# Eleven more matmuls on a zero tile around TensorE's branch, in the opening of an attention and feed-forward kernel

## The reference

```python
q, k, v = x @ Wq.T, x @ Wk.T, x @ Wv.T * sigmoid(x @ Wg.T)   # 16 query heads, 4 key heads, 8 wide
q, k = rotary(rms_norm(q)) * q_gain, rotary(rms_norm(k))
# each head is split in halves; two causal softmax attentions a1, a2
y = concat([a1 - lam * a2, a1 + lam * a2])
x = layernorm(x + y @ Wo.T)
gf = global_net(mean of x over the tokens)                    # small MLP
for _ in range(3):
    tf = coupling_net(x_ffn)                                  # four dense layers
    x_ffn = x_ffn + coupling(gf, tf) * twist(x_ffn)
out = layernorm(x + x_ffn)
```

## Time and profile before

| what | value |
|---|---|
| runs | 264.01, 264.76 and 271.02 us |
| median | 264.76 us |
| profiled execution, its own time | 266.62 us |
| its span, first to last instruction | 264.8 us |
| TensorE busy, share of the span | 234.5 us, 89% |
| VectorE | 206.1 us, 78% |
| ScalarE | 218.8 us, 83% |
| GpSimd | 95.9 us, 36% |
| mean granted clock of TensorE | 0.962 of 2.4 GHz |

### The profile page before, as it was taken

How to read it: one execution, slowest core, us unless ns; L and a number is a source line. 1 busy time by engine, 2 the same in 40 slices (tenths; PEclk the granted TensorE clock), 3 DMA queues, 4 the chain that set the end, 5 groups by cost and what they waited for, 6 DMA issues and landing times.

```text
span 264.8 us, 10915 instructions
## 1 busy us (share of the span) xinstructions
PE 234.5 (89%) x4240; PEld 127.9 (48%) x4240; DVE 206.1 (78%) x747; ACT 218.8 (83%) x316; POOL 95.9 (36%) x225
## 2 busy tenths in 40 slices
PE   8459799997799999999999999899998899998980
PEld 3143456654465564565665554544643222223980
DVE  1789667997878899899899989943442967999992
ACT  3367699997968999999999999999766697777785
POOL 7730323444534354444453553522203000000573
PEclk9957799999979999999999999999999999999997
DMA  4304252461717535346264353381201345651045
GB/s 120 85 1 77 46 121 62 88 133 32 159 42 102 112 85 120 82 96 128 70 119 101 82 114 73 67 156 16 60 12 43 80 102 136 160 122 37 24 138 159
DMA packets 58223, 23.60 MB, mean 89 GB/s; under 512 B 42929, under 2 KB 56145, under 8 KB 58193
## 3 DMA queue, kind: packets, MB, share of 16 engines
q1 hardware_dynamic: 57904, 23.16, 40.9%
q10 hardware_dynamic: 288, 0.02, 0.1%
HBM read 4.96 MB, written 2.10 MB: 27 GB/s over the span
## 4 chain that ended last, share of the span: by engine, by line
PE 31%; DVE 25%; issue 15%; DMA 11%; POOL 10%; ACT 4%; SPq 1%; POOLq 1%; DVEq 1%; ACTq 0%
DMA qk<-parts 9%; PE S L767 7%; DVE roped L1206 3%; PE S L777 2%; PE O L648 2%; DVE rest L1234 2%; PE S L808 2%; POOL root_sq L1603 2%; PE O L635 2%; DVE X L1326 2%; DVE stats L1331 2%; ACT h L1037 2%; DVE parts L1232 2%; POOL root_sq L1595 2%; DVE parts L1236 2%
## 5 line engine op out<-in xcount | busy, mean ns | idle before, releaser
L948 ACT ACTIVATE probs_past<-S 128x1024 f32<-128x1024 f32 x64 | 64.0, 1037 | 3.9 <-PE S L506 3.8
L948 ACT ACTIVATE probs_late<-S 128x1024 f32<-128x1024 f32 x64 | 62.3, 1028 | 4.0 <-PE S L537 3.2
L635 PE MATMUL O<-probs_past,values 128*32 128x512 f32 x256 | 35.0, 618 | 1.2 <-issue 0.6
L648 PE MATMUL O<-probs_late,mixed 128*32 128x128 f32 x512 | 27.4, 286 | 0.0
L648 PE MATMUL O<-probs_late,values 128*32 128x128 f32 x512 | 27.1, 282 | 0.0
L1466 DVE SCALAR_TENSOR_TENSOR cY<-coup,ratio,Y 128x256 f32<-128x256 f32 x48 | 21.1, 481 | 6.3 <-ACT coup L1046 3.8
L767 PE MATMUL S<-X,cn_w 128*128 128x512 f32 x48 | 25.0, 627 | 0.0
L1595 POOL TENSOR_TENSOR root_sq<-estimate 128x40 f32<-128x40 f32 x16 | 6.8, 424 | 40.8 <-DVE estimate L1194 36.7
L516 PEld LDWEIGHTS S<-qk 32*128 32x128 bf16 x512 | 7.6, 92 | 27.9 <-issue 27.9
L1206 DVE TENSOR_TENSOR roped<-rotated,rstd 128x128 f32<-128x128 f32 (+1 forms) x64 | 15.6, 299 | 6.8 <-POOL rstd L1605 6.8
L506 PE MATMUL S<-qk 32*128 32x512 bf16 x128 | 13.7, 412 | 7.9 <-DMA qk<-parts 7.2
(11 more groups left out here) (190 smaller groups left out, 585.3 us busy)
## 6 DMA issues: line engine op xcount, KB each, us to landing
Y<-X SPq DMA_DIRECT2D x48, 128.0 KB, 2.3
xT_in<-in_xT SPq DMA_DIRECT2D x16, 128.0 KB, 2.7
x_res<-in_x SPq DMA_DIRECT2D x16, 128.0 KB, 2.4
out<-result SPq DMA_DIRECT2D x16, 128.0 KB, 1.9
qk<-parts SPq DMA_TRANSPOSE x15, 4.9
future_in<-in_future SPq DMA_DIRECT2D x1, 176.0 KB, 2.8
w_o<-in_w_o SPq DMA_DIRECT2D x2, 64.0 KB, 2.4
cn_w<-in_cn_w SPq DMA_DIRECT2D x2, 64.0 KB, 2.1
```

The lines of the kernel that those rows point to most:

```text
L635: mm = pe.matmul(O[32 * g:32 * g + 32, :], values[p][:, 0, g, s, at:at + 32], probs_past[:, s, g, :], start=m == 0, stop=False)
L648: mm = pe.matmul(O[32 * g:32 * g + 32, :].rearrange("p (r n) -> p r n", r=R)[:, :, QUARTER * to:QUARTER * to + QUARTER], weights, probs_la ...
L948: act.activation(dst, S[TILE_BUFFER[n]][:, :, :], ACT.Exp).then_inc(exp_done[n], 1)
```

## The change

The matmuls on the zero tile before the branch become ten instead of four, and those at the head of the attention body nine instead of four. The edit of the second stands in `attention`, so it is in both bodies. Nothing else is changed: no wait, no tile, no other engine.

```diff
             def attention(general):
-                keep_awake(4)
+                keep_awake(9)
                 pe.wait_ge(n_["ident16_ready"], 2)
                 pe.wait_ge(n_["first_parts_ready"], 3)
                 turn_first_keys()
...
             is_bounded = pe.value_load(bounded[0:1, 0:1], min_val=0, max_val=1)
-            keep_awake(4)
+            keep_awake(10)
             with pe.If(is_bounded < 1):
```

## The result

The time went up: 267.7 us median of four runs (266.86 to 271.78) against 264.38 of four runs of the kernel before, ratio 1.012 with a 95% interval of 1.007 to 1.017. The forecast was 264.6 us, in a range of 262.9 to 266.3. The ratios in this document leave out runs that lie over 1.5% above the fastest run of the same kernel; this kernel's runs scatter over more than that, so all runs are given as well.

A forecast was written before the change was run, and what follows sets the result against it. The chain that ended last runs over VectorE, then the first DMA transpose; TensorE's opening holes are off it. Added matmuls 0, clock over first transposes -0.10 on the path: 264.76 - 0.1 = 264.66, say 264.6 us, range 262.9 to 266.3.

The forecast's parts named there:

- the base on which the sum stands: Whole kernel: median of the runs before the change, 264.76 us, from which the forecast gain was subtracted.
- The zero matmuls cost nothing in the opening: TensorE's opening: added matmuls fit beside the branch and VectorE's chain, cost 0, at worst 0.02 us.
- One sign of being wrong: Opening: the prediction is wrong if the branch's end, at about 11.06 us, moves by over 0.5 us.
- held back by ten matmuls: Rival at the branch: taken only once the zero matmuls before it have started, giving 265.5 us; chance 0.08.
- The clock over the first transposes: Opening, twelve transposes: if TensorE's clock holds, they save 0.58 us on TensorE; otherwise nothing.
- The forecast's likelier case: Opening: the clock holds over the first transposes, gaining 0.1 us; chance 0.40, against 0.35 for the clock falling anyway.
- The path gains 0.10 us: Second set of transposes: VectorE's line 1242 releases them, so only 0.10 of 0.58 us arrives; 0.47 if they speed up too.
- The DMA transpose takes its 6.69 us at any clock: First DMA transpose, from 22.78 us to TensorE's release at 29.51: claimed to last 6.69 us whatever the clock.
- the second rival: Opening and beyond: the clock holds throughout and the second low stretch goes too, giving 262.5 us; chance 0.12.
- one of its signs of being wrong: After the first DMA transpose: the prediction is wrong if the second low stretch at 29.9 us disappears.
- Six before the branch 0, five behind it 0: Sum's terms for the added matmuls before and behind the branch: each costs 0, bounds 0 and +0.02 us.
- Theory L: Experiments' layout theory: added instructions move TensorE's 16 KB program fetches; one beside qk's last DMA transpose delays it, 6.6 against 5.3 us.

The follow-up runs named there:

- e6: The change plus 80 more matmuls (160 instructions) in the body that is not executed: 264.34 us, ratio 0.999 to the kernel before.
- e4: The change plus 112 more matmuls in the body that is not executed, code 256 instructions further on than before: 266.94 us, ratio 0.991.
- e9: The change once more, unedited, against the kernel before: 267.11 us (6 runs), ratio 1.015.
- e3: The kernel before plus sixteen more matmuls in the body that is not executed, taken code 32 instructions further on: 267.63 us, ratio 1.009.
- e11: The change with 160 unexecuted instructions, measured a second time: 265.84 us (6 runs).
- e15: The kernel before, unedited, profiled again for the third time: profiled execution 268.59 us.
- e1: The kernel before with only the six matmuls before the branch added (ten there, four behind): 268.88 us, ratio 1.010.
- e5: The change plus 32 more matmuls (64 instructions) in the body that is not executed, 96 from the old place: 267.63 us.
- e8: The change plus nine more zero matmuls in the hole where TensorE waits for the last transpose of qk: 265.85 us, ratio 1.010.

## Why the prediction was wrong

The forecast was 264.6 us and the four runs gave 267.7, so it missed by 3.1 us. It missed in two terms: the base on which the sum stands, and a cost for which it has no term.

**The base was too low: 1.8 us of the miss.** The sum starts from 264.76 us, the median of three runs. Ninety-nine runs of the same kernel have a median of 266.57. The width that the range gives to the scatter, 0.8 us, is that of two of the three runs; the third, 271.02, was left out of it, and the 99 spread from 260.9 to 273.6. No row of the trace was read wrongly here; three runs were too few. The rest of the miss is the difference between the two kernels, a gain of 0.1 us in the forecast and a loss of 1.1 us by the medians of all their runs (267.65 of ten against 266.57).

**The zero matmuls cost nothing in the opening: right.** Their durations, the branch beside them, and the margin before the first transposes came out as worked out (10 in 2.33 us, 9 in 2.12, transposes at 15.12). One sign of being wrong did show: the end of the branch moved by more than 0.5 us, from 11.06 to 10.43. It moved forwards, since the projection of sequence 0 took 1.10 us instead of 1.83; the branch itself took 3.92 us instead of 3.82, and in all eighteen profiles it starts between 6.5 and 7.3 us and takes 3.5 to 4.7. It was not held back by ten matmuls.

**The clock over the first transposes: right.** The forecast's likelier case held, eight transposes in 0.61 us against 0.65 forecast. It was not luck of one execution: they take 0.61 to 0.64 us in eight of the nine profiles with the whole change (1.06 in e6), and 1.06 in all seven with the opening of before.

**The path gains 0.10 us: right in kind, small in size.** The second set of transposes is released by line 1242 and stays at the lower clock. From the first transpose to VectorE's copy of line 1250 it takes 3.65 us (15.12 to 18.77) instead of 3.83, so 0.18 us arrive where 0.10 was forecast. In two other profiles of the change (e4, e9) the second set runs at the upper clock too, and 0.6 us arrive; the forecast had 0.47 for that. The first DMA transpose is issued at 22.46 us in the profile, 0.32 earlier, of which 0.14 is VectorE's own earlier start. Over all profiles it is 22.66 us on the mean for the seven that execute the opening of before and 22.42 for the nine with the whole change, 0.25 us earlier.

**"The DMA transpose takes its 6.69 us at any clock": wrong as a fixed duration.** This sentence took a duration from one row; that the clock has no part in it stands untested. In the changed kernel the first transpose lands after 5.6 us, and the same transfer takes 4.8 to 7.1 us over all profiles. With the shorter hole of 1.14 us, the clock did not fall behind it and the second low stretch was missing: the second rival's event, by a way that the forecast had ruled out, and one of its signs of being wrong. The low stretch that starts between 28 and 31 us is missing in five of the nine profiles with the change and in one of the seven with the opening of before. Over the same profiles the third DMA transpose is issued at 43.85 us on the mean with the opening of before (seven, 42.6 to 45.0) and at 42.65 with the change (nine, 41.2 to 44.1), so the opening gains 1.2 us there and not 0.1.

**The step that failed: the sum has no term for the length of TensorE's program.** "Six before the branch 0, five behind it 0" counts the time of the instructions and not their place. Twenty-two executed and ten unexecuted instructions move everything behind them by 32, and that costs more than the opening gains: about 1.1 us by the mean of e3's runs against those beside them, where the sum has nothing. It is shown by e3, which executes what the kernel before executes and has its shortest of 12 runs at 266.50 us, where the kernel before has 39 of 99 runs under 266. The change has none of 10 there, e4 five of 12. The mean of the change's ten runs is 267.7 us against 266.5 for the 99 runs of the kernel before, ratio 1.005 [1.001, 1.009] by resampling the runs; e3's is 267.9, ratio 1.005 [1.002, 1.008]; against the 29 runs beside it alone it is 1.004 [1.000, 1.008], so the size is uncertain. Compared at equal place, the executed matmuls bring +0.1 us (99 against 12 runs, if 0 and 256 are the same place), -0.2 (12 against 10) and -1.0 us (14 against 18). None of the three is clear of the scatter.

**What the place acts on.** The kernel before lands its last transpose in time in three of four profiles; all profiles at 12, 20 and 32 instructions further on are late. Late means 1.3 us for the transfer and a longer hole, behind which the clock falls. The whole is 2.9 us, of which the filled hole gives back about 1.1; about 0.5 is assigned to neither. The mean over all runs moves by less, since the kernel before has late runs as well and the change starts ahead.

```profile
q8 instruction: 11, 0.18, 1.1%
qk<-parts SPq DMA_TRANSPOSE x6, 6.3
...
qk<-parts SPq DMA_TRANSPOSE x8, 4.9
...
q8 instruction: 4, 0.07, 0.8%
```

Queue 8 fetches 16 KB at a time (0.18 MB in 11). In the middle, where TensorE runs in its loop, it fetches nothing, and all eight transposes take 4.8 to 4.9 us; outside it there are eleven and four fetches, and transposes of up to 6.7 us. At the last transpose of the changed kernel one fetch lies between 174.3 and 175.6 us, 4.1 to 5.4 us after the issue:

```profile
q8 instruction: 1, 0.02, 4.6%
```

All twelve late last transposes have a fetch in this stretch. Of the six in time four have none, but e4 and e11 have one there and land after 5.3 and 5.2 us. The other transposes say more. The eighteen profiles hold 270 of them; sorted by when a fetch beside them starts, counted from their issue:

| fetch of queue 8 beside the transpose | transposes | they land after, us |
|---|---|---|
| none | 150 | 4.8 to 4.9 |
| one, starts before the issue or within 0.3 us | 12 | 4.8 to 5.0 |
| one, starts after 0.6 to 1.1 us | 13 | 5.1 to 5.7 |
| one, starts after 1.5 to 3.6 us | 11 | 5.6 to 6.2 |
| one, starts after 4.3 to 4.9 us | 65 | 4.8 to 4.9 (15), 6.5 to 6.9 (50) |
| two | 19 | 5.0 to 7.1 |

No transpose without a fetch lands later than 4.91 us, and the later the fetch starts, the later the transpose lands, up to the 15 that a late fetch leaves alone. The last transpose of the kernel before has its fetch 0.66 us after the issue and lands after 5.28; that of e3, which executes the same and lies 32 instructions further on, has it after 4.59 us and lands after 6.57. The unchanged kernel has a fetch 4.46 us after the issue too in one of its four profiles, e15, and is late there. So the fetch goes with the delay and its size, and the place of the code changes how often one falls late beside the last transpose. What is missing is a run that moves a fetch and nothing else, and a reason why some late fetches cost 1.7 us and others nothing. Theory L also forecast the wrong places (e1 and e5 were to be spared). It is well supported, not shown. The Trainium skill, "Runtime: NRT & Kernel Launch", "Instruction fetch mechanics", says that the sequencer fetches 16 KB blocks of 256 instructions while it executes and that crossing a boundary is mostly hidden. The block size agrees with queue 8; whether the crossing is hidden for TensorE itself no run here was made to show, and for a transfer beside it the table speaks against it. The same page of the Trainium skill made e4 possible: 256 instructions further on, the late landing was gone in the one profile taken.

**A version that may beat both.** The change with 160 unexecuted instructions has a mean of 264.9 us over 18 runs, ratio 0.994 [0.990, 0.998] to the 99 runs of the kernel before, and was under 266 us in 14 of 18. It is 0.6%, the place was picked as the best of several, and its second series (e11) was only 0.3 us under the kernel before. It hangs on a place of code that the next edit moves. Filling the hole before the last transpose (e8) should be the sturdier repair; no run tried it at another place, and its six runs are 0.5 us under the kernel before beside them, within the scatter.

## What to carry to other kernels

An instruction that costs nothing where it stands still makes the program longer. Before a small gain or loss is put down to what an edit executes, add the same number of instructions where they are never executed, and look whether the time moves as well. Measure a kernel against itself first: here one program's runs spread from 260.9 to 273.6 us and its four profiles had two modes, so four runs beside four runs said 264.4 against 267.7 where the means differ by 1.2 us. Where a total is undecided, cut the trace at an event near the suspected place: the time from the last transpose's issue to the end told the late from the timely landings without an exception.

## What was not expected of the hardware

The same DMA transpose of 2560 packets of 256 bytes lands after 4.8 to 4.9 us in the loop in every profile and after up to 7.1 us outside it, and never after more than 4.91 us without an instruction fetch beside it. At the last transpose, TensorE's clock went to 0.50 in all eleven profiles with an empty hole of 1.89 to 2.65 us, for 3.4 to 6.8 us; it stayed at 1.00 in the six with a hole of 0.64 to 0.95 us, and in the one where zero matmuls filled it.
